# Short score stacks copied within themselves, and the FFN of each entry inside the attention loop

## The reference

```
q = Wq @ layernorm(x) + bq ; k = Wk @ ctx + bk ; v = Wv @ ctx + bv      # 128 channels = 16 heads x 8
dot = q . k / sqrt(8), masked: mask*dot - (1-mask)*1e6                   # 16 heads, 256 x 256 scores each
x = x + tanh(g_xattn) * (softmax(dot) * mask) @ v
y = layernorm(x)                                                         # over the 256 positions
x = x + tanh(g_ffn) * bitlinear(silu(bitlinear(y, W1)), W2)              # 256 -> 1024 -> 256
# bitlinear: the input is rounded to 8 bits per row (scale 127 / max|row|), the weight to {-1, 0, 1} * mean|W|
```

## Time and profile before

| what | value |
|---|---|
| runs of the kernel | 302.21, 302.62 and 304.54 us, median 302.62 |
| the profiled execution: span from its first to its last instruction | 298.2 us; its time outside the span isn't listed |
| granted TensorE clock, mean over the span | 0.805 of full |
| busy: TensorE, VectorE, ScalarE, GpSimd | 173.6, 169.8, 121.6, 68.9 us |
| DMA | 20477 packets, 19.89 MB |

### The profile page before, as it was taken

The page is one execution under the profiler, slowest core; times in us unless marked ns, Lnnn a source line. Parts: engine busy times, 40 slices in busy tenths (PEclk is TensorE's granted clock), DMA queues, the critical chain, the costliest instruction groups (busy, mean ns, idle before and its releaser), DMA issues.

```text
span 298.2 us, 3874 instructions
## 1 busy us (share of the span) xinstructions
PE 173.6 (58%) x1429; PEld 86.1 (29%) x1432; DVE 169.8 (57%) x334; ACT 121.6 (41%) x153; POOL 68.9 (23%) x117
## 2 busy tenths in 40 slices
PE   0520071087100187888706899729888897768763
PEld 0220041032000043443303445315444443224532
DVE  4725043089000375867802999927999942549993
ACT  1230165011000036644343656505565677665661
POOL 5334006000000346024332332201404140201100
PEclk9955558557555577979955999978999999977999
DMA  3899758965886305558545155520000000000111
GB/s 112 227 124 182 113 119 118 108 61 103 135 88 136 104 4 69 61 65 103 79 81 75 19 66 62 61 31 0 6 0 6 0 7 0 2 1 0 54 36 53
DMA packets 20477, 19.89 MB, mean 67 GB/s; under 512 B 2776, under 2 KB 19416, under 8 KB 20426
## 3 DMA queue, kind: packets, MB, share of 16 engines
q1 hardware_dynamic: 18411, 17.51, 35.6%
q0 software_dynamic: 1344, 2.07, 6.4%
q10 hardware_dynamic: 704, 0.07, 0.2%
HBM read 5.59 MB, written 1.07 MB: 22 GB/s over the span
## 4 chain that ended last, share of the span: by engine, by line
PE 26%; SPq 22%; DMA 22%; DVE 16%; POOL 5%; issue 5%; ACT 3%; POOLq 0%
DMA q_st<-negm_p 13%; SPq L232 10%; SPq L217 7%; PE ps_pv L878 7%; PE ps_max L845 6%; DMA k_st<-in_L_ffn_W 6%; PE ps_exp L861 5%; DVE rec L639 4%; DMA mask_b<-in_mask_Bx1x_fk 3%; DVE hs L649 3%; PE ps_mix L784 2%; DVE mx L622 1%; SPq L257 1%; DVE x_sb L677 1%; SPq L194 1%
## 5 line engine op out<-in xcount | busy, mean ns | idle before, releaser
L622 DVE TENSOR_REDUCE mx<-ps_max 128x2 f32<-128x512 f32 x128 | 83.2, 685 | 47.6 <-PE ps_max L845 47.2
L845 PE MATMUL ps_max<-k_st,q_st 96*128 96x256 bf16 x256 | 55.7, 308 | 45.5 <-DVE mx L622 32.2
L501 ACT ACTIVATE probs<-ps_exp 128x1024 f32<-128x1024 f32 x64 | 65.4, 1023 | 36.3 <-PE ps_exp L861 35.5
L861 PE MATMUL ps_exp<-q_st,k_st 99*128 99x256 bf16 x256 | 41.4, 286 | 21.2 <-DMA q_st<-negm_p 20.8
L878 PE MATMUL ps_pv<-probs,v_aug 128*32 128x256 f32 x512 | 42.8, 407 | 4.0 <-ACT pv_sb L509 2.4
L845 PEld LDWEIGHTS ps_max<-k_st,q_st 96*128 96x128 bf16 x256 | 19.7, 104 | 81.8 <-DVE mx L622 56.5
L861 PEld LDWEIGHTS ps_exp<-q_st,k_st 99*128 99x128 bf16 x256 | 24.2, 102 | 33.0 <-DMA q_st<-negm_p 21.6
L379 POOL TENSOR_TENSOR negm<-negm,negm_p 16x256 f32<-16x256 f32 x8 | 5.3, 662 | 99.2 <-DVE negm_p L632 50.6
L541 DVE BATCH_NORM_STATS2 stats<-x_sb 128x6 f32<-128x256 f32 x8 | 3.4, 426 | 33.4 <-DMA x_sb<-in_x 33.3
L639 DVE RECIPROCAL rec<-ps_mix 128x256 f32<-128x256 f32 x8 | 14.1, 1758 | 7.7 <-PE ps_mix L784 7.7
L437 ACT ACTIVATE qk<-ps_mix,bq_s 128x512 f32<-128x512 f32 x2 | 1.4, 688 | 39.3 <-PE ps_mix L759 39.3
(11 more groups left out here) (119 smaller groups left out, 224.3 us busy)
## 6 DMA issues: line engine op xcount, KB each, us to landing
q_st<-qk_p SPq DMA_DIRECT2D x27, 128.0 KB
k_st<-qk_p SPq DMA_DIRECT2D x24, 128.0 KB
k_st<-in_L_ffn_W SPq DMA_DIRECT2D x2, 1024.0 KB, 16.2
q_st<-probs SPq DMA_DIRECT2D x9, 128.0 KB
c_sb<-in_ctx SPq DMA_DIRECT2D x4, 256.0 KB, 8.4
mask_b<-in_mask_Bx1x_fk SPq DMA_DIRECT2D x2, 512.0 KB, 7.8
out<-x_sb SPq DMA_DIRECT2D x8, 128.0 KB, 1.7
k_st<-probs SPq DMA_DIRECT2D x6, 128.0 KB
```

The source lines that it names most:

```text
L501: nc.scalar.activation(probs[:, s % RING, :], ps_exp[:, s % 2, :], ACT.Exp).then_inc(S["exp_done"], 1)
L622: nc.vector.tensor_reduce(mx[:, b % 2, :].rearrange("t (c h) -> t h c", c=2)[:, h, :], ps_max[:, hh, :].rearrange("t (c s) -> t c s", c=2) ...
L845: ins = nc.tensor.matmul(ps_max[:, hh, c * T:(c + 1) * T], q_at(b, h)[0:K_MAX, c * 128:(c + 1) * 128], k_at(b, h)[0:K_MAX, :], start=True, ...
L861: ins = nc.tensor.matmul(ps_exp[:, g % 2, o:o + T], k_at(b, h)[0:K_EXP, c * 128:(c + 1) * 128], q_at(b, h)[0:K_EXP, :], start=True, stop=True)
```

## The change

- The stacks have 84 rows: the shift rows follow the mask rows directly, and there is no padding. The places in the stacks are three, used in turn.
- `first_rows` brings each part once into blocks 0 to 2 (six transfers of 128 KB per pair). `wide_rows` copies from these blocks to the others inside the stack: two transfers of 24 rows for k, four of 8 or 16 rows for q.
- The maxima are negated by the reduction itself (`negate=True`), split on GpSimd, turned by two TensorE transposes as 48 rows, and brought into the stack by one transfer on GpSimd's queue.
- Pair 1 is projected inside the loop. AHEAD is 13. FFN weights are loaded from ScalarE's queue and clipped on GpSimd.
- `gather_heads` takes positions to partitions (pv_sb as the stationary side, a selection matrix of 72 columns moving), so 32 reciprocals per partition do, and the mask multiplies these; `turn_back` transposes the result, and VectorE adds it to x. `attend` accumulates two quads into one bank; the values have 32 columns a head.
- Each entry's FFN stands in the loop, 15 to 20 slots behind its first exp slot. SiLU is taken as (1 + tanh(u/2)) * u, the factor 2 folded into scales; y and h are quantised on GpSimd.
- All users of `ps_max` (max scores, v, gather, turn back, down) take its two banks in turn in one order, `vec_order`; `mix_order` and `exp_order` do so for `ps_mix` and for the two halves of `ps_exp`.

```diff
-    AHEAD = 14
-    SHIFT_ROW = 96
+    AHEAD = 13
+    SHIFT_ROW = MASK_ROW + PARTS * PARTS
+    PLACES = 3
+    VH = 32
+    O_COLS = (HP + 1) * HD
...
+        PAIR_EVENTS = {"stats": -16, "xn": -14, "k": -13, "q": -13, "hi": -12, "mid": -11, "hi_rows": -12, "mid_rows": -11,
+                       "lo_rows": -10, "wide_rows": -9}
+        V_AT = 8
+        ENTRY_EVENTS = {"split": 8 - AHEAD, "shift": 9 - AHEAD, "shift_rows": 9 - AHEAD, "att": 10, "back": 11,
+                        "y": 12, "y_max": 13, "y_quant": 13, "y_turn": 14, "up": 15, "h": 16, "h_quant": 16, "h_turn": 18,
+                        "down": 20}
+        W_EVENTS = {"w_total": 2 - AHEAD, "w_round": 3 - AHEAD, "w_turn1": 5 - AHEAD, "w_turn2": 7 - AHEAD}
...
+            use += [(w, p) for p in range(1, PAIRS) for w, at in PAIR_EVENTS.items() if s == max(16 * p - AHEAD + at, -AHEAD)]
...
-        PAIR_EVENTS = {"stats": (-5, 8), "xn": (-4, 9), "q": (-3, 10), "k": (-2, 12), "hi": (-1, 14), "mid": (0, 15),
-                       "v": (21, 37), "hi_rows": (0, 14), "mid_rows": (5, 20), "lo_rows": (8, 23)}
-        ENTRY_EVENTS = {"shift": HP - AHEAD, "sel": HP + 3, "y_stats": HP + 5, "y_quant": HP + 7, "y_turn": HP + 8}
...
+            def first_rows(p, part):
+
+                done = ("qk_hi", "qk_mid", "qk_lo")[part]
+                for o, st, arrived in ((1, k_st, k_first), (0, q_st, q_first)):
+                    sp.wait_ge(S[done], 2 * p + 2 - o)
+                    sp.dma_start(st[HD * part:HD * (part + 1), p % PLACES, :, :], qk_p[:, o, part, :]).then_inc(arrived[p], 16)
+
+            def wide_rows(p):
+
+                at = p % PLACES
+                W = PARTS * HD
+                sp.wait_ge(k_first[p], 16 * PARTS)
+                for i in (1, 2):
+                    sp.dma_start(k_st[W * i:W * (i + 1), at, :, :], k_st[0:W, at, :, :]).then_inc(k_wide[p], 16)
+                sp.wait_ge(q_first[p], 16 * PARTS)
+                for to, of, n in ((3, 1, 2), (5, 0, 1), (6, 2, 1), (7, 0, 2)):
+                    sp.dma_start(q_st[HD * to:HD * (to + n), at, :, :], q_st[HD * of:HD * (of + n), at, :, :]).then_inc(q_wide[p], 16)
...
+            def clip_weights(w):
+                pool.wait_ge(S["w_rounded"], w + 1)
+                nc.gpsimd.tensor_scalar(w_q[w], w_q[w], ROUND - 1.0, ROUND + 1.0, ALU.max, ALU.min).then_inc(S["w_quant"], 1)
+
+            def shift_parts(b):
+
+                pool.wait_ge(S["vec_out"], vec_at[("max", 2 * HP * (b + 1) - 1)] + 1)
...
+                link(nc.gpsimd.tensor_copy(nparts[:, :, 0, :], m))
+                link(nc.gpsimd.tensor_tensor(nres[:], m, nparts[:, :, 0, :], ALU.subtract))
+                link(nc.gpsimd.tensor_copy(nparts[:, :, 1, :], nres[:]))
+                nc.gpsimd.tensor_tensor(nparts[:, :, 2, :], nres[:], nparts[:, :, 1, :], ALU.subtract).then_inc(S["shift_split"], 1)
+
+            def shift_rows(b):
+                pool.wait_ge(S["mix_out"], mix_at[("shift", b)] + 1)
+                dst = q_st[SHIFT_ROW:SHIFT_ROW + PARTS, b // 2 % PLACES, :, (b % 2) * T:(b % 2 + 1) * T]
+                pool.dma_start(dst, negm_p[:]).then_inc(S["shift_in"], 16)
...
+            def quantise_h(b):
+
+                at = [hs[:, b, i:i + 1] for i in range(5)]
+                step = ys[:, b, 3:4]
+                pool.wait_ge(S["h_max"], b + 1)
+                link(nc.gpsimd.tensor_scalar(at[1], at[0], step, 1e-5, ALU.mult, ALU.max))
+                link(nc.gpsimd.tensor_tensor(at[2], at[1], minus_one[:], ALU.pow))
+                link(nc.gpsimd.tensor_scalar(at[3], at[2], step, 127.0, ALU.mult, ALU.mult))
+                if b >= 1:
+                    pool.wait_ge(S["mix_full"], mix_at[("h_turn", b - 1)] + 1)
+                nc.gpsimd.tensor_scalar(hq[:], hb[:], at[3], ROUND, ALU.mult, ALU.add).then_inc(S["hq_ready"], 1)
...
+            def attention_out(b):
...
+                link(nc.vector.reciprocal(rec[:], o_ps[:, :, HP * HD:O_COLS]))
...
+            def silu_max(b):
+
+                at = exp_at[("up", b)]
+                dve.wait_ge(S["tanh_done"], b + 1)
+                nc.vector.scalar_tensor_tensor(out=hb[:], in0=hb[:], scalar=1.0, in1=ps_exp[:, at % 2, :],
+                                               op0=ALU.add, op1=ALU.mult).then_inc(S["up_out"], 1)
+                dve.wait_ge(S["up_out"], b + 1)
+                nc.vector.tensor_reduce(hs[:, b, 0:1], hb[:], AX_X, ALU.max, apply_absolute_value=True).then_inc(S["h_max"], 1)
...
+            def gather_heads(b):
+                bank = take_vec(("att", b))
...
+                for i in range(2 * DC):
+                    c, f = i // 2, i % 2
+                    ins = nc.tensor.matmul(bank[:, i * O_COLS:(i + 1) * O_COLS], pv_sb[:, f, c * 128:(c + 1) * 128], sel[:],
+                                           start=True, stop=True)
+                ins.then_inc(S["vec_full"], 1)
```

More of the change, by code:

```diff
@@ new lines, in gated_block @@
+        vec_order, mix_order, exp_order = [], [], []
+        for s in range(-AHEAD, LAST):
+            if 0 <= s < SLOTS:
+                exp_order.append(("exp", s))
+            if s + AHEAD < SLOTS:
+                vec_order += [("max", 2 * (s + AHEAD)), ("max", 2 * (s + AHEAD) + 1)]
+            vec_order += [u for u in events(s) if u[0] in ("v", "att", "back", "down")]
+            mix_order += [u for u in events(s) if u[0] in ("q", "k", "shift", "y_turn", "h_turn")]
+            exp_order += [u for u in events(s) if u[0] == "up"]
@@ new lines, in turn_back, with turn_shift @@
+            def turn_back(b):
+                bank = take_vec(("back", b))
+                pe.wait_ge(S["vec_out"], vec_at[("att", b)] + 1)
+                for c in range(DC):
+                    ins = nc.tensor.transpose(bank[:, c * 128:(c + 1) * 128], attT[:, c * 128:(c + 1) * 128], ident[:])
+                ins.then_inc(S["vec_full"], 1)
+            def turn_shift(b):
+                take_mix(("shift", b))
+                pe.wait_ge(S["shift_split"], b + 1)
+                for c in range(DC):
+                    ins = nc.tensor.transpose(ps_mix[0:PARTS * H, c * 64:(c + 1) * 64].bitcast(BF16),
+                                              nparts[:, c].rearrange("t i h -> t (i h)"), identb[:])
+                ins.then_inc(S["mix_full"], 1)
```

975 lines of the change are left out of this document (467 added, 508 removed).

## The result

The changed kernel takes 341.54 us (median of 4 runs, 334.28 to 344.92), the kernel before 302.47 on the same chip: 1.113 times as long (95% interval 1.104 to 1.123). The forecast was 247, range 226 to 272. The profiled execution took 344.92 us, with a span of 342.8. A second set of its runs gave 341.61. (Ratios are of undisturbed runs alone, so one can differ from the quotient of two medians.)

The account below looks back on a forecast made before the run. The prediction saw transfers bounding the part before slot 0, and VectorE and TensorE nearly full in the loop. Its terms, 77 + 12 + 100 + 22 + 32 = 243 us of span, plus 4.4, gave 247 us, range 226 to 272.

Parts of the forecast that it names:

- slots 3 to 9: Loop before any FFN work: 7 slots at 1.75 us each, 12 us.
- narrow 13: Prologue: a pair's six narrow transfers, 0.79 MB, take 13 us, between 7.1 at 111 GB/s and 13.2 at 60.
- wide 12: Prologue: a pair's copies inside the stack, 1.57 MB, take 12 us, between 6.8 and 22.
- rival (c): Prologue: copying inside the stack is as slow as before, 39.7 us a pair; 295 us in all, chance 0.05.
- 2048 columns cost 3.1 (at most 5.8): Prologue: cost in us of a GpSimd clip of FFN weights, scaled up from 386 ns for 256 columns.
- 19.0 per entry, bounds 17.5 and 21: Loop: us for an entry of 8 slots with the FFN in it, TensorE being the bound.
- VectorE's 16.0: Loop: VectorE's work per entry in us, from 15.7 before, less what leaves, plus 3.34 that comes.
- TensorE's 17.5: Loop: TensorE's work per entry in us, from 14.7 before, with 2.7 for the FFN's steps.
- I give the new one 1.5: Loop: us per entry for waits, also for the exp bank the up projection holds; the old entry had 1.3.
- hides under 19: Loop: GpSimd's share, about 8 us an entry and 5.5 of pair work, adds no time to the 19 us entry.
- Rival (d): Loop: TensorE and VectorE take turns over banks, their times add to 33.5 us an entry; 320 us in all, chance 0.05.
- 32 of shift stalls gone: Loop: us saved because two late shift transfers, 19.1 and 12.9, no longer queue behind stack rows and padding.

## Why the prediction was wrong

By the forecast's own dates, against the profiled run:

| step of the forecast | forecast | measured | off by |
|---|---|---|---|
| first max scores | 38 | 52.1 | 14 |
| from there to slot 0 | 29 | 40.8 | 12 |
| slot 0 to slot 3's max scores | 10 | 13.6 | 4 |
| slots 3 to 9 | 12 | 26.2 | 14 |
| slots 10 to 50 | 100 | 145.0 | 45 |
| slots 51 to 62 | 22 | 30.3 | 8 |
| tail | 32 | 34.8 | 3 |
| sum (span) | 243 | 342.8 | 100 |

(Slot 10 at 132.69 and slot 51 at 277.67. The median of the runs lies 1.3 below this span, where the forecast added 4.4; so 100 on the span are 94.5 on the time.)

**The transfers.** The start at 12.5 was right (12.2). The terms narrow 13 and wide 12 failed: 18.5 and 21.3 (43 and 74 GB/s), together 39.9 us, as long as the 39.7 of the earlier trace rows. That is rival (c) for pair 0, which gave 52 for the first max scores. Its 105 for slot 3's max scores came true as well (106.5), but by luck: with the clips on VectorE they run at 93.5. The bounds were drawn from rates of other transfers. The 21.3 are within their slow end, 22, which was put aside for a row "nearer the quick end"; the only row of a like thing, SyncE's own span from first issue to first max scores, was not taken as a bound. The Trainium skill's rule on the spread over engines ("DMA: Bandwidth & Descriptors", "Why a DMA increments its semaphore by 16 and not by 1") gave an estimate of 9.4 to 18, and the run with narrow transfers alone, which the rule has on fewer engines, filled pair 0 as quickly. For pair 1, without mask rows beside them, the wide rows took 15.7 (90.4 to 106.1), inside that estimate.

**The clips.** "A one-input GpSimd operation takes 386 ns for 256 columns, ... so 2048 columns cost 3.1 (at most 5.8)" failed: 7.09. The mechanism, pair 1 and the split queued behind them, was right, and the experiment gives the term its price, 11.5 us of the whole. The row scaled up was a cast of 16 partitions without a scalar; the operation has two scalars and 128 partitions. The same scaling failed for y: 1241 ns for 256 columns. The Trainium skill, "GPSIMD Engine Reference", section "When to use GPSIMD", puts two-input work on GpSimd at about half the speed of VectorE and calls one-input work "roughly line-rate"; the measurement differs: 7092 against 694 ns, 1241 against 423, 1118 against 753, and only 477 against 477 is as the page has it. The measurement decides.

**Pair 1 and slot 3's stop.** A 5 us stop in slot 3 was forecast, and 6.35 came. Right, 29 us later than said.

**The loop.** The term "19.0 per entry, bounds 17.5 and 21" failed, with 45 of the 100 us. Its parts are unequal. VectorE's 16.0 was right (16.1). In slots 33 to 49 TensorE was busy 21.8 us an entry for the 17.5 and idle 4.8 for the 1.5; the two together, 4.3 and 3.3, are the 7.6 by which the entry's 26.6 is over 19.0. TensorE's 17.5 was right at full clock: with dummies in the loop alone, 45.98 us over 18 slots are 20.4 an entry; 64 dummies in them took 8.5 us, 3.8 an entry, which leaves 16.7. What failed was "I give the new one 1.5" for all waits, and that the work would be done at full clock. The first comes from the order of work, and the second came with the stops. The step "hides under 19" looked at the sum of GpSimd's work (it is busy only 38% of the time), not at what stands in front of what: "GpSimd's share ... hides" was said of a queue whose first element waits for TensorE and whose second is waited for by TensorE. The experiments put numbers on it: 21.0 us for the order of two GpSimd operations, and 17.1 for keeping the clock up in the kernel as changed, the dummies' own time already paid (once the stops are fewer, no clear gain). At full clock an entry with dummies is 22.9 (181.18 to 227.04 for 16 slots): 16.7 of work, 3.8 of dummies and 2.4 of waits that are left. Without dummies the same slots took 23.3 an entry, at a clock of 0.93. No run had a full clock without dummies there, so whether 19.0 could be had in this order of work stays open.

**Rival (d)** had the right sign and a near time, 320, but its mechanism, all of TensorE's and VectorE's work in turns, 33.5 an entry, isn't what happened: an entry of 26.6 holds 21.8 of TensorE and 16.1 of VectorE, so they overlap. The sign that was named for (d), each busy half an entry, didn't show: they were busy 82% and 61% of it. "TensorE busy over nine tenths" was half true, in stretches, for the wrong reason. "No shift wait over 3 us" failed at slot 0, for the transfer (5.5), and at two turns that waited for the split (4.8 at 83.1 and 3.2 at 142.3).

**Slots 3 to 9, 51 to 62 and the tail.** Slots 3 to 9 were priced at 1.75 each; they ran at a clock of 0.50 until 130 us, where a slot with nothing beside the attention takes 2.8. Slot 4, with entry 1's turn and its wait of 1.3, took 4.7, slot 8, with the values of pair 1, 4.5, and slot 6, with the projections of pair 2, 7.4. The forecast had counted these projections among slots 10 to 50. The forecast took clock from the earlier trace rows at 1.00 and nowhere asked what would hold it there. The tail was nearly right (34.8 for 32) and so was its chain; the table load (one) and the short reciprocal (358 ns for "0.2 to 0.4") were right.

**Slips in the working.** 60 GB/s over eight engines are 7.5 an engine, not 7.1, so the estimate for the wide rows ends at 17.5 and not at 18. Rival (d) takes off 99 us where the sum has 97, and would give 322. And "32 of shift stalls gone" counts the lengths of two transfers, while in the kernel before TensorE stood 18.7 us behind them:

```profile
158.87 1.03 PE L861 MATMUL ps_exp<-q_st,k_st 99*128 99x256 bf16 x4 [12.00 <-DMA q_st<-negm_p]
...
199.52 1.04 PE L861 MATMUL ps_exp<-q_st,k_st 99*128 99x256 bf16 x4 [6.67 <-DMA q_st<-negm_p]
```

The forecast itself isn't built on any of the three.

**What stays open.** Of the 94.5 us between forecast and measurement, repairs and dummies give back 46 (341.6 to 295.3). Of the other 48 in the quickest of these kernels, 10 stand at slot 0 (77.4 for 67, behind transfers that end 13 later than forecast), 36 in the 63 slots (180.3 for 144; its 192 dummies have 28.5 us of TensorE's busy time) and 2 in the tail. No run has pair 0's copies without the mask rows beside them, and none takes away the stops behind SiLU (six of up to 1.9 us in the changed kernel), which needs another bank.

## What to carry to other kernels

When work moves to an engine with room, write its queue out in order beside the queue of the engine that waits for it, and look for an operation that waits for that engine in front of one that it waits for. Sums of busy time don't show this: here a one-line change of place was worth 21 us with GpSimd at 38%. And where TensorE is the bound, short stops have two prices, the stops themselves and the slots at half clock that can follow; a forecast at full clock needs a reason why the clock stays up.
